# Expert rows that queue up over several groups: 85 tiles for 113, an indirect store by token, a convolution moved to TensorE, and the last sums on VectorE

## What is computed

```python
h = layernorm(x) * (1 + ca) + sa
u = causal depthwise convolution of h over time, 4 taps, + conv_b
dt, Bm, Cm = split(u @ xproj_w.T)                  # 128, 16, 16 columns
delta = softplus(dt @ dtproj_w.T + dtproj_b)
s_t = exp(delta * A) * s_{t-1} + delta * Bm * u    # 512 channels x 16 states
x = x + ga * (sum_n(s_t * Cm) + u * D_skip)
h = layernorm(x) * (1 + cb) + sb
logits = tanh(h @ Wg1.T) @ Wg2.T                   # 8 experts
x = x + gb * sum over the best two experts of softmax score * (silu(h @ Wup.T + bup) @ Wdown.T + bdown)
```

## Time and profile before

| | us |
|---|---|
| three timed runs | 1375.56, 1375.56, 1377.5 (median 1375.56) |
| the profiled execution's own time | 1375.48 |
| its span, first to last instruction | 1373.7 |
| PE, DVE, ACT, POOL busy | 1193.0, 1085.5, 937.0, 995.8 |
| first and last scan start | 47.0, 1238 |
| last matmul ends | 1350 |

### The profile page before, as it was taken

The page is one execution under the profiler, slowest core; times in us unless marked ns, Lnnn a source line. Parts: engine busy times, 40 slices in busy tenths (PEclk is TensorE's granted clock), DMA queues, the critical chain, the costliest instruction groups (busy, mean ns, idle before and its releaser), DMA issues.

```text
span 1373.7 us, 20313 instructions
## 1 busy us (share of the span) xinstructions
PE 1193.0 (87%) x5980; PEld 809.1 (59%) x5980; DVE 1085.5 (79%) x1428; ACT 937.0 (68%) x1790; POOL 995.8 (72%) x788
## 2 busy tenths in 40 slices
PE   8869768779978786799988989999999998999992
PEld 4457635556645554566655656766666665666551
DVE  4998899999999999899989859899888884393100
ACT  4754876689687865787879757777697765464330
POOL 1675776886767778999686679999888988765132
PEclk9999969999999997899999989999999999999996
DMA  6586343566413333565233354675544566655432
GB/s 203 172 267 191 118 132 119 172 193 193 141 47 100 105 116 106 141 187 174 94 102 106 137 153 129 202 228 164 162 123 140 153 201 178 182 145 140 150 120 76
DMA packets 121857, 204.87 MB, mean 149 GB/s; under 512 B 27012, under 2 KB 35204, under 8 KB 120728
## 3 DMA queue, kind: packets, MB, share of 16 engines
q1 hardware_dynamic: 109464, 169.89, 39.4%
q0 software_dynamic: 12288, 33.69, 9.2%
HBM read 123.82 MB, written 79.71 MB: 148 GB/s over the span
## 4 chain that ended last, share of the span: by engine, by line
PE 46%; POOL 11%; DVE 10%; ACT 10%; issue 9%; DMA 1%; DVEq 0%; POOLq 0%; ACTq 0%
PE pb L1833 8%; PE pb L1931 6%; PE pb L1906 6%; DVE ACC L1586 5%; PE pb L1936 5%; PE pb L1913 4%; DVE H L1561 3%; POOL DB L1125 3%; PE pb L1930 3%; ACT pb L1345 2%; PE pb L1889 2%; POOL xdr L1077 2%; POOL DB L1119 2%; PE pb L1904 2%; PE pb L1852 2%
## 5 line engine op out<-in xcount | busy, mean ns | idle before, releaser
L1119 POOL TENSOR_TENSOR DB<-DU,BR 128x1024 f32<-128x1024 f32 x222 | 530.1, 2401 | 154.5 <-DVE H L1561 146.2
L1586 DVE SCALAR_TENSOR_TENSOR ACC<-pb,CTM,ACC 128x512 f32<-128x512 f32 x512 | 372.1, 727 | 41.8 <-PE pb L1833 39.9
L1345 ACT ACTIVATE pb<-DELP,AN 128x512 f32<-128x512 f32 x448 | 305.5, 686 | 108.2 <-DVE H L1561 107.0
L1833 PE MATMUL pb<-ID,H 128*128 128x128 f32 x2048 | 312.5, 284 | 74.2 <-DVE ACC L1586 42.8
L1833 PEld LDWEIGHTS pb<-ID,H 128*128 128x128 f32 x2048 | 246.8, 145 | 171.1 <-issue 58.6
L1561 DVE TENSOR_TENSOR_SCAN H<-pb,DB 128x512 f32<-128x512 f32 x256 | 309.7, 1211 | 23.3 <-ACT pb L1345 17.4
L1561 DVE TENSOR_TENSOR_SCAN H<-pb,ST,DB 128x512 f32<-128x512 f32 x192 | 244.4, 1273 | 29.2 <-ACT pb L1345 15.3
L1931 PE MATMUL pb<-WD,GT 128*128 x226 | 131.9, 667 | 0.0
L1906 PE MATMUL pb<-WU,XTS 128*128 x452 | 131.7, 415 | 0.0
L1431 ACT ACTIVATE YO<-pb,SCR 128x512 f32<-128x512 f32 x113 | 77.2, 683 | 73.6 <-PE pb L1936 73.4
L1913 PE MATMUL pb<-WU,XTS 128*128 x452 | 119.0, 387 | 0.0
(11 more groups left out here) (225 smaller groups left out, 1879.4 us busy)
## 6 DMA issues: line engine op xcount, KB each, us to landing
XS<-xdr SPq DMA_DIRECT2D x113, 256.0 KB
ydr<-YO SPq DMA_DIRECT2D x113, 256.0 KB
BR<-bscr SPq DMA_DIRECT2D x112, 256.0 KB
xdr<-ZX SPq DMA_DIRECT2D x69, 258.0 KB
ACC<-in_x SPq DMA_DIRECT2D x16, 512.0 KB, 4.5
DU<-in_x SPq DMA_DIRECT2D x7, 1024.0 KB
x1s<-ACC SPq DMA_DIRECT2D x24, 256.0 KB, 2.8
ZX<-x1s SPq DMA_DIRECT2D x24, 256.0 KB
```

The lines of the kernel that those rows point to most:

```text
L1119: eng.tensor_tensor(DB[:, i % NDB:i % NDB + 2], DU[:, c % 2, r:r + 2], BR[:, n % 2:n % 2 + 1].to_broadcast([128, 2, CT]), ALU.mult).then_i ...
L1345: eng.activation(DA[i % NDA][:], DEL[:, c % 2, r], ACT.Exp, scale=AN[:, r, n:n + 1]).then_inc(S["da"], 1)
L1586: eng.scalar_tensor_tensor(out=acc, in0=banks[bank_of["flip", c, n, r]][:], scalar=1.0 if n < 0 else CTM[:, c % 2, j, st:st + 1], in1=acc, ...
L1833: t = eng.transpose(b[:, dt * 128:dt * 128 + 128], src[:, dt, r * 128:r * 128 + 128], ID[:])
```

## The change

- **Queues.** Groups stand in three queues: half chunks 0 to 7 (four groups), 8 to 14 (four groups), and 15. An expert has its own region of `xdr` for a whole queue, and rows that don't fill a tile wait for the queue's next group. All groups but a queue's last run only the number of tiles that are sure to be full, `max(0, 2 * depth(g) - 7)` up to there; the last runs what the worst split may need, `2 * depth(g) + 7`. That gives 1, 8, 8, 22; 1, 8, 8, 18; and 11 tiles: 85.
- A new sort step `c2` of 11 to 15 small dependent instructions on VectorE finds each tile's expert and first row; SP reads that row and the score's column from memory into registers for each `xl`, and loads the tile and, in a second DMA, 128 pairs of 8 bytes with score and token number.
- **Store by token.** `yst` becomes an indirect DMA on GpSimd's queue that writes each row at its token's place in a `ydr` of 2 x 4096 rows; rows that belong to no token are dropped. The gathers go; `yg` becomes two plain loads a token tile from SP.
- **Sums.** `za` (the two experts' rows), `zm` and `fin` move to VectorE. They can begin only when a whole queue's tiles are stored; 6 of each stand in front of the last scan's position, 26 of each behind.
- **Convolution.** `pe_tiles(c)` is all four tiles in chunks 1 to 7, so `conv`, `cvs` and `cva` go, outside chunk 0.
- Buffers: XS 4 deep for 3, YO 3 for 2, TH 2 for 1, GB 2 for 1; ZX and Z go (the sums use what chunk 6 leaves in DU and DEL). 37 zero stores to `xdr` for 69, and 16 indirect ones that close the two long queues. `PLACES` and `BANKS` are new throughout. Positions above 16384, before and after: `xt` 16 and 23, `up` 18 and 25, `dn` 21 and 27, `gt` 11 and 13. The last ones: `dq` 18104 and 18738, `out` 18634 and 19232. Behind the last `dq` of group (14,) (17708) and its last `yst` (17924) stand `yg` for 16 token tiles, the first at 17968, and the 11 tiles of group (15,).

```diff
-GROUPS = ((0, 1), (2, 3, 4, 5), (6, 7, 8, 9), (10, 11), (12, 13), (14,), (15,))
-NXD = 3
-NXS = 3
-NYO = 2
+QUEUES = (((0, 1), (2, 3), (4, 5), (6, 7)), ((8, 9), (10, 11), (12, 13), (14,)), ((15,),))
+GROUPS = tuple(group for queue in QUEUES for group in queue)
+HTC = D + 2 * NE
+NXS = 4
+NYO = 3
...
 def pe_tiles(c):
-    return {0, 1, 2, 3} if c in (1, 2, 3) else set()
+    return {0, 1, 2, 3} if c else set()
...
+def depth(g):
+    return sum(len(tokens(x)) for x in groups_of(queue_of(g)) if x <= g)
...
+def taken(g):
+    return 2 * depth(g) + 7 if last_in(g) else max(0, 2 * depth(g) - 7)
...
 def n_tiles(g):
-    return (256 * len(tokens(g)) + NE * 127) // 128
+    return taken(g) - (0 if first_in(g) else taken(g - 1))
...
-    return at + [("xs", g), ("sx", g)]
+    if last_in(g) and filled(queue_of(g)):
+        at += [("zs", g)] + [("zr", g, e) for e in range(NE)]
+    return at
...
# SP, xl
-                    eng.dma_start(XS[:, m % NXS], xdr[g % NXD][i * 128:i * 128 + 128, 0:D]).then_inc(S[f"d_xl{m % NXS}"], 16)
+                    at_row = row_of(m, g)
+                    eng.dma_start(XS[:, m % NXS], xdr[queue_of(g)][bass.ds(at_row, 128), 0:D]).then_inc(S[f"d_xl{m % NXS}"], 16)
+                    eng.dma_start(SCR[:, m % NSC], xdr[queue_of(g)][bass.ds(at_row, 128), bass.ds(col_of(m), 2)]).then_inc(
+                        S[f"d_xl{m % NXS}"], 16)
# SP, yg
+                    if t == 0 and way == 0 and first_in(g):
+                        last = tile_no(groups_of(queue_of(g))[-1] + 1, 0) - 1
+                        for r in range(NYO):
+                            eng.wait_ge(S[f"d_y{r}"], 16 * ((last - r) // NYO + 1))
+                    if way == 0 and turn:
+                        eng.wait_ge(S["fin"], b - 1)
...
+                    eng.dma_start(z_tile(g, t, way), ydr[r0:r0 + 128, :]).then_inc(loaded, 16)
# GpSimd, yst
+                    eng.wait_ge(S["ye"], m + 1)
+                    eng.indirect_dma_start(out=ydr[:, :], out_offset=bass.IndirectOffsetOnAxis(ap=SLOT_ROW[m % NSC], axis=0),
+                                           in_=YO[:, m % NYO], in_offset=None, bounds_check=2 * T - 1,
+                                           oob_is_err=False).then_inc(S[f"d_y{m % NYO}"], 16)
# VectorE
+                elif what == "za":
+                    eng.wait_ge(loaded, 32 * (turn + 1))
+                    eng.tensor_tensor(z_tile(g, t, 0), z_tile(g, t, 0), z_tile(g, t, 1), ALU.add).then_inc(S["za"], 1)
+                elif what == "zm":
+                    eng.tensor_tensor(z_tile(g, t, 0), z_tile(g, t, 0), GB[:, tokens(g)[t][0] // 4 % 2], ALU.mult).then_inc(S["zm"], 1)
+                elif what == "fin":
+                    eng.tensor_tensor(to, to, z_tile(g, t, 0), ALU.add).then_inc(S["fin"], 1)
```

More of the change, by code:

```diff
@@ L359, in place_of, with queue_of, groups_of, first_in @@
     return tokens(group_of(cs)).index((cs, j))
[L362 to L364 removed]
+def queue_of(g):
+    return next(q for q in range(len(QUEUES)) if GROUPS[g] in QUEUES[q])
+def groups_of(q):
+    return [g for g in range(len(GROUPS)) if queue_of(g) == q]
+def first_in(g):
+    return g == groups_of(queue_of(g))[0]
+def last_in(g):
+    return g == groups_of(queue_of(g))[-1]
+def depth(g):
+    return sum(len(tokens(x)) for x in groups_of(queue_of(g)) if x <= g)
+def taken(g):
+    return 2 * depth(g) + 7 if last_in(g) else max(0, 2 * depth(g) - 7)
+def n_tiles(g):
+    return taken(g) - (0 if first_in(g) else taken(g - 1))
+def filled(q):
+    return len(groups_of(q)) > 1
+def region(q):
+    return 128 * (depth(groups_of(q)[-1]) + filled(q))
+def rows_in(q):
+    return NE * region(q) + 128 * (NE - 1)
+def counted(g):
+    return n_tiles(g) > 0 and not last_in(g)
 def most_tiles():
     return max(n_tiles(g) for g in range(len(GROUPS)))
+def all_tiles():
+    return sum(n_tiles(g) for g in range(len(GROUPS)))
+def zeroed():
+    return [(q, i) for q in range(len(QUEUES)) for i in range(NE * region(q) // 128 if filled(q) else 0, rows_in(q) // 128)]
 def n_pairs(g):
@@ L432, in experts @@
         at += [(what, g, i) for i in tiles_of(g, q) for what in ("dn", "dq", "ye", "yst")]
-    for t, (cs, j) in enumerate(tokens(g)):
-        at += [("gbl", cs // 4)] if cs and cs % 4 == 0 and j == 0 else []
-        at += [("yg", g, t, 0), ("yg", g, t, 1)] + ([("xr", g, t)] if bounced(cs) else [])
-        at += [("zm", g, t), ("fin", g, t), ("out", g, t)]
+    for x in groups_of(queue_of(g)) if last_in(g) else ():
+        for t, (cs, j) in enumerate(tokens(x)):
+            at += [("gbl", cs // 4)] if cs and cs % 4 == 0 and j == 0 else []
+            at += ([("xr", x, t)] if bounced(cs) else []) + [("za", x, t), ("zm", x, t), ("fin", x, t), ("out", x, t)]
+    of = [(x, t) for x in groups_of(queue_of(g)) for t in range(len(tokens(x)))] if last_in(g) else []
+    at += [("yg", x, t, way) for x, t in of for way in range(2)]
     return at
@@ L685, in tile_expert, with row_of, col_of @@
         def tile_expert(g, i):
-            return nc.values_load(EID[0:1, g, i:i + 1], engines=[mybir.EngineType.PE], min_val=0, max_val=(NE - 1) * 1024,
+            m = tile_no(g, i)
+            return nc.values_load(EID[0:1, m:m + 1], engines=[mybir.EngineType.PE], min_val=0, max_val=(NE - 1) * 1024,
+                                  skip_runtime_bounds_check_because="the number of an expert is clamped to the last one on the chip")
+        def row_of(m, g):
+            return nc.values_load(ROW[0:1, m:m + 1], engines=[mybir.EngineType.SP], min_val=0, max_val=rows_in(queue_of(g)) - 128,
+                                  skip_runtime_bounds_check_because="a tile's first row is worked out from counts on the chip")
+        def col_of(m):
+            return nc.values_load(COL[0:1, m:m + 1], engines=[mybir.EngineType.SP], min_val=D, max_val=HTC - 2,
                                   skip_runtime_bounds_check_because="the number of an expert is clamped to the last one on the chip")
@@ L697, in x1_tile, with z_tile, turn_of_z, turn_of @@
             cs, j = tokens(g)[t]
-            return ZX[:, back_no(g, t) % 2] if bounced(cs) else acc_tile(cs // 2, 2 * (cs % 2) + j)
+            if not bounced(cs):
+                return acc_tile(cs // 2, 2 * (cs % 2) + j)
+            return DEL[:, (NC - 2) % 2, back_no(g, t) % 4]
+        def z_tile(g, t, way):
+            return DU[:, (NC - 2) % 2, 2 * (back_no(g, t) % 2) + way]
+        def turn_of_z(g, t):
+            return S[f"d_g{back_no(g, t) % 2}"], back_no(g, t) // 2
+        def turn_of(g, t):
+            r = back_no(g, t)
+            return S[f"d_v{r % 4}"], S[f"d_p{r % 4}"], r // 4
+        SLOT_ROW = [SCR[:, i, 1:2].bitcast(u32) for i in range(NSC)]
         def rows_of(g, t):
@@ L899, in _ @@
                     eng.wait_ge(S["fin"], back_no(g, t) + 1)
-                    eng.dma_start(out[rows_of(g, t), :], x1_tile(g, t)).then_inc(S[f"d_o{back_no(g, t) % 2}"], 16)
-            for q in range(2):
-                eng.wait_ge(S[f"d_o{q}"], 16 * 2 * NC)
+                    eng.dma_start(out[rows_of(g, t), :], x1_tile(g, t)).then_inc(turn_of(g, t)[1], 16)
+            for g in range(len(GROUPS)):
+                for t in range(len(tokens(g))):
+                    _, stored, turn = turn_of(g, t)
+                    eng.wait_ge(stored, 16 * (turn + 1))
             eng.wait_ge(S["d_bw"], 16 * NC)
```

618 lines of the change are left out of this document (344 added, 274 removed), and 276 rows, old and new, of the table PLACES.

## The result

| | before | after |
|---|---|---|
| median of 4 runs each, us | 1376.53 | 1310.64 (1308.79 to 1312.63) |
| ratio | | 0.9521, 95% interval 0.9503 to 0.9539 |
| profiled execution, its span | 1375.48, 1373.7 | 1310.42, 1308.7 |
| first scan, last scan, last matmul | 47.0, 1238, 1350 | 43.7, 1132.3, 1292.5 |
| scan stage, and from last scan to end | 1191, 135.6 | 1088.6, 176.4 |

The forecast was 1318 us, made of 47, 1104, 165 and 1.8. It is 7 us above the median: the head (everything up to the first scan) took 3.3 and the scan stage 15.4 less, the tail 11.4 more. So part of the nearness is luck: two errors of opposite sign cancel.

A forecast was written before the change was run, and what follows sets the result against it. The prediction took VectorE to set the scans' pace first and TensorE later, then a tail of matmuls. Head 47, scan stage 1104, tail 165 and 1.8 outside the span gave 1318 us, range 1270 to 1366.

The forecast's parts named there:

- VectorE's content, 1032.5 us forecast: Scan stage: VectorE's 1043.3 us less 40.9 (conv) and 12.2 (gg), plus 26.3 (sums) and 16.0 (sort).
- 18 x 1.46 = 26 us: Scan stage, VectorE: 18 sums ahead of the last scan, each priced at the 1.46 us of conv.
- The lower bound, 0.73: Scan stage: lowest price per VectorE sum, from a 128x512 instruction with PSUM; 13 us for all 18.
- Its share, 0.935 forecast: Scan stage: VectorE's busy share taken from the earlier kernel's first half; 1032.5 / 0.935 = 1104 us.
- TensorE: 111 + 33.6 = 144.6 us: Tail: earlier 111 us of matmuls plus 33.6 us of additional ones behind the last scan.
- the second sum of the forecast: Tail: last matmul 144.6, scaling and indirect store 4, loads 3.4, six sums 4, store 2.5: 159 us.
- 4.6 us a token tile: Tail: two loads, an x1 load and a store, 1.05 MB at 228 GB/s; 74 us for 16 token tiles.
- 1 (share 0.973): Scan stage: VectorE denser still, stage 1061 us, total 1275 us; chance 0.14.
- 2 (7 us a token tile): Tail: late sums, one token tile at a time, set the end; tail 199 us, total 1352; chance 0.15.
- 3 (the lock): Scan stage: each of 18 VectorE sums also pays a whole GpSimd instruction, 29 us, total 1349; chance 0.09.
- 4 (the indirect store holds the scans): Scan stage: 56 indirect stores on GpSimd's queue each wait for their result, 62 us, total 1380; chance 0.08.
- 5 (coupling, share stays at 0.875): Scan stage: VectorE's idle time comes from five engines' coupling; stage 1179 us, total 1393; chance 0.09.

The follow-up runs named there:

- e1: Changed kernel with the convolution of chunks 4 to 7 back on VectorE, GpSimd and ScalarE: 1363.29 us, against the changed kernel's 1310.64.
- e4: Changed kernel with the 48 additions and products of the first queue's 16 token tiles on GpSimd, not VectorE: 1335.19 us.
- e7: Changed kernel with the sums of the first six token tiles placed behind the last scan, like the other 26: 1317.21 us.
- e12: Changed kernel with half the width of VectorE's 192 additions in chunks 4 to 6, so part is not computed: 1309.47 us.
- e3: Changed kernel with two more 256-column products of zeros in the up-projection of the 60 tiles placed ahead of the last scan: 1357.39 us.
- e2: Changed kernel leaving out two of four up-projection products in the 60 tiles placed ahead of the last scan: 1305.7 us.
- e9: Changed kernel with the convolution of chunks 4 to 7 moved back and two more products of zeros in 60 tiles' up-projection: 1393.55 us.
- e10: Changed kernel with the down-projection of the second tile of four late pairs issued behind the next pair's up-projections: 1308.32 us.
- e6: Changed kernel with four pairs of buffers, not two, for the second and third queue's sums, loaded two token tiles earlier: 1312.89 us.
- e5: Changed kernel leaving out two of four up-projection products in the last 25 tiles, placed behind the last scan: 1296.81 us.
- e8: Changed kernel with tile results stored in order by SyncE's plain transfer, not GpSimd's indirect one, so rows land elsewhere: 1306.59 us.

## Why the prediction came out right

**Where the gain lies.** As forecast: the scan stage won, the tail gave some back. Forecast were 88 and 30 us; 102 and 41 were measured, and 3.3 came from the head, which I had called unchanged. Nothing was tried on the head, so its 3.3 us stay unexplained.

**VectorE's content, 1032.5 us forecast, 1012.8 measured.** The mis-sized term is the sums: 18 x 1.46 = 26 us. I priced them by the nearest row in kind, `conv`. Only 15 of them ran ahead of the last scan, in 13.6 us, 0.91 each, of which 0.69 is their own and the rest the lock (below). The lower bound, 0.73, taken from the rows with PSUM, was nearer. That is 12.7 of the 19.7 us. The sort's small steps came to 26.4 us for 12.4, 14 more where I had 16, and `gg` to 12 less, as forecast. The other 5 us I can't put to a term. The 28 `conv` were right: bringing them back added 37.0 us where I had 40.9.

**Its share, 0.935 forecast, 0.931 measured.** Right, and with it the stage: the 15 us by which 1104 was too long are 21 us of content too many less 5 of share. But the division gave the right number for half a reason. Adding to VectorE costs time (e1: 37 us of work and more on GpSimd and ScalarE, 51 us), taking from it doesn't (e4, e7, e12: 11, 12 and 45 us of work; the stage moved by +8, 0 and -1). The same holds for TensorE (e3: 51 us of work, 41 us; e2: 35 us less, 5). Over the second half of the scans TensorE and VectorE are both near nine tenths, and they wait for each other, so that relief of one turns into waits for the rest. What relief of both at once would bring was not tried.

**The convolution.** 55 us onto TensorE, 41 off VectorE by my count: by busy time alone a poor trade. It is worth 53 us (e1), by far the larger part of the gain. I forecast the sum of both and never priced them apart. That it pays because 28 tiles had left TensorE holds only in part: with 51 us of work put back on TensorE it is still worth 36 (e9 against e3). What it would be worth with all 113 tiles, 146 us more of TensorE, was not tried.

**The tail, 165 forecast, 176.4 measured.** The range held, but this is where the sum went wrong. The step that failed is "TensorE: 111 + 33.6 = 144.6 us"; it is 160.2. By the line groups between last scan and last matmul TensorE did 29 down products (21 before), 25 ups and 25 turns. I had put 27 and 23, from the positions; the engine came to the last scan two tiles behind its list, 2 x 2.33 + 2 x 0.44 = 5.5 us. The second part is holes: 8.5 us of idle in front of the pairs' turns and downs, 1.5 before, mostly since two-tile pairs of a short last queue have no other pair to fill them: 7.0 us more, of which e10 took out some 4. The third is the lower clock behind the longest hole, 1.6 us. And 1.0 us is where I began to count: I took the 111 us from 1239, 1 us behind the start of the last scan, and the 160.2 us run from its start. Together 15.1 of the 15.6 us. The end behind the last matmul, 16.2 us, had some 14 in the second sum of the forecast.

**The sums' own chain** was forecast at 4.6 us a token tile, and measured at 4.5: from 1235.8 to 1303.9 us for the last 16. That the two agree is partly luck: 4.6 came from bandwidth, but at first the sums come two token tiles at a time, at 1235.8, 1244.2, 1255.9 and 1267.6 us, and 11.7 us is TensorE's pace for a pair of tiles. They start later than thought, the second queue's last store lying 95 and not 86 us behind the last scan, because the matmuls do. The two chains do end together, as the forecast had it, but they are not separate: cutting the sums' (e6) gives 2 us, and cutting TensorE's moves both (e5). The last two token tiles can't be loaded before the last expert tile is stored, and that store follows the last matmul. The tile loads and the sums' loads also share SyncE's list; what that adds was not tested.

**The rivals.** 1 (share 0.973): the stage's mean is 0.931, and e12 says that less work for VectorE doesn't shorten it. 2 (7 us a token tile): no, 4.5. 3 (the lock): it is there, and small; its rows follow. 4 (the indirect store holds the scans): by 5 us at most, by the waits and by e8, where 62 had been put. But e4 shows its mechanism at work in the tail as soon as something that waits for a load stands in front of the stores. 5 (coupling, share stays at 0.875): wrong on the number; on what the share is, e12 speaks for it.

The lock, in the changed kernel's timeline, GpSimd's product and then VectorE's sum:

```profile
1070.92 1.28 POOL L1253 TENSOR_TENSOR DB<-DU,BR 128x512 f32<-128x512 f32 x1
```

```profile
1070.82 1.94 DVE L1829 TENSOR_TENSOR DELP<-DELP,DU 128x512 f32<-128x512 f32 x1
```

The sum began 0.1 us ahead of the product and took 1.94 us where its median is 0.69: its own time and the whole product's 1.28. Four of the 15 sums ahead of the last scan were stretched like that (1.26, 1.94, 1.58 and 1.43 us), 3.5 us in all; rival 3 had put 29. The Trainium skill ("SBUF — State Buffer", section "Who interferes with whom") calls the port pair of the two engines an exclusive lock, and these rows agree. What the forecast needed was how often the two meet, and that is no matter of the rule.

**The clock.** TensorE's granted clock in the two halves of the scan stage was 0.88 and 0.96, below the 0.91 and 0.98 of before, as forecast. The stage came out within 15 us of its forecast all the same; what the clock cost in it no run separates (in e1 it fell further, to 0.87). In the tail it cost 1.6 us, behind a hole.

## What to carry to other kernels

Divide an engine's content by its share to forecast a change that adds work or moves it, but don't read the quotient as leverage: in this kernel, with two engines near nine tenths, added work showed and removed work did not. A part that looks like a loss by busy time (55 us on, 41 off) can be the one that pays, and pays more if another part has made the room (53 us against 36); price them apart. And when tiles move behind the last scan, count the holes between them as well as their matmuls: with a single chain of pairs left, each wait for a neighbour engine stands uncovered until something is put in front of it.

## What the runs showed of the hardware that was not expected

- An fp32 product with 256 columns shows as two records of 0.379 us, but they overlap: two take 0.70 and four 1.13, so one product occupies TensorE for 0.43 us where products follow each other. Record length times count overstates such a row of products by three quarters.
- A sum of two SBUF tiles of 128x512 took 0.69 us on VectorE, 0.72 in the mean of all 96 sums and products with the lock included; on GpSimd it took 1.27 (e4).
- SyncE, which reads a register from memory between a tile's two loads, issued them 1.0 us apart where one issue takes 0.33:

```profile
1226.06 0.33 SPq L982 DMA_DIRECT2D XS<-xdr  x1
1227.06 0.33 SPq L983 DMA_DIRECT2D SCR<-xdr  x1
```

  So such a read costs about 0.67 us of SyncE's time, near the 0.70 that I had put as its bound. TensorE's turns (L2070) and their weight loads waited for a tile's load 2.0 and 3.8 us in the whole run.
- The indirect store by token number cost GpSimd 1.06 us a tile. In the tail it cost no more than a plain one that could be told from scatter: with plain stores (e8) the tail was 1 us shorter.
- One hole of 1.47 us was followed by 4 us at a granted clock of 0.57 (1280.3 to 1284.3 us), and four records of L2087 took 1.60 us for 1.13. Four holes of 1.03 us before it, 11.7 us apart, brought no such stretch.
